# A gated cross-attention and expert layer: the attention groups' work in a new order on all engines

## What is computed

```python
h  = layernorm(x)
q  = rope(h @ Wq.T + bq) * 16**-0.5;  k = rope(ctx @ Wk.T + bk);  v = ctx @ Wv.T + bv
p  = softmax(where(causal and within 128, q @ k.T, -inf))          # for each of 16 heads
x  = x + tanh(g_xattn) * ((p @ v) @ Wo.T + bo)
xf = layernorm(x)
ri = concat(xf, [mean, std, min, max, l2, share of zeros])          # six router statistics
probs = softmax(gelu(ri @ r1_w.T + r1_b) @ r2_w.T)                  # then the best two, capacity 140 an expert
x  = x + tanh(g_ffn) * (sum of the chosen experts' silu MLPs + 0.05 * weighted adapters)
```

## Time and profile before

| | us |
|---|---|
| median of 3 runs | 757.16 (756.15 to 764.54) |
| the profiled execution's own time | 759.58 |
| its span in the profile | 757.7 |
| TensorE matmul busy | 650.4 (86%) |
| VectorE busy | 526.0 (69%) |
| ScalarE busy | 405.2 (53%) |
| GpSimd busy | 323.7 (43%) |

### The profile page before, as it was taken

How to read it: one execution, slowest core, us unless ns; L and a number is a source line. 1 busy time by engine, 2 the same in 40 slices (tenths; PEclk the granted TensorE clock), 3 DMA queues, 4 the chain that set the end, 5 groups by cost and what they waited for, 6 DMA issues and landing times.

```text
span 757.7 us, 17528 instructions
## 1 busy us (share of the span) xinstructions
PE 650.4 (86%) x5275; PEld 513.0 (68%) x5275; DVE 526.0 (69%) x1548; ACT 405.2 (53%) x1569; POOL 323.7 (43%) x340
## 2 busy tenths in 40 slices
PE   8788988989889898899988112899999999999992
PEld 4455655656656566566654101599999999999992
DVE  6765786867778677785988889677778645445441
ACT  2377787887878878788683555022222222222220
POOL 3443462544526435262112000435665665665643
PEclk9999999999999999999798555699999999999997
DMA  5610020200202002010101601169888988888821
GB/s 183 219 37 26 26 74 2 74 27 25 73 0 73 26 25 73 0 49 1 50 2 50 243 0 25 35 200 259 255 250 257 268 260 264 266 236 264 274 44 15
DMA packets 57852, 85.83 MB, mean 113 GB/s; under 512 B 11452, under 2 KB 28468, under 8 KB 57652
## 3 DMA queue, kind: packets, MB, share of 16 engines
q1 hardware_dynamic: 47588, 74.37, 29.7%
q0 software_dynamic: 9216, 9.76, 7.9%
q10 hardware_dynamic: 976, 0.89, 0.4%
HBM read 72.30 MB, written 12.69 MB: 112 GB/s over the span
## 4 chain that ended last, share of the span: by engine, by line
PE 51%; ACT 20%; DVE 17%; issue 7%; DMA 2%; POOL 1%; ACTq 1%; DVEq 1%; POOLq 0%
PE pair L1014 19%; ACT arena L1320 10%; PE bank L1024 10%; DVE arena L1493 4%; PE pair L1655 3%; PE pair L1646 3%; PE bank L1609 2%; ACT arena L583 2%; PE pair L515 2%; PE bank L1036 2%; ACT arena L1269 2%; PE bank L1597 1%; PE pair L1641 1%; PE bank L1003 1%; DVE we L1474 1%
## 5 line engine op out<-in xcount | busy, mean ns | idle before, releaser
L1320 ACT ACTIVATE arena<-pair,arena 112x112 f32<-112x112 f32 x512 | 174.5, 362 | 28.2 <-DVE arena L1493 19.5
L1014 PE MATMUL pair<-arena,we 128*128 128x140 f32 x1024 | 138.0, 283 | 0.7 <-ACT arena L927 0.6
L905 POOL DMA_INDIRECT rows_out<-arena,slot_row x64 | 94.4, 1475 | 95.8 <-DVE arena L958 82.6
L1014 PEld LDWEIGHTS pair<-arena,we 128*128 128x128 f32 x1024 | 128.5, 190 | 1.2 <-issue 1.2
L935 ACT ACTIVATE arena<-pair 128x140 f32<-128x140 f32 x160 | 45.9, 287 | 149.6 <-PE pair L1014 149.6
L970 DVE SCALAR_TENSOR_TENSOR arena<-arena,pair 128x140 f32<-128x140 f32 x160 | 47.5, 297 | 98.4 <-ACT arena L935 97.5
L1320 ACT ACTIVATION_READ_ACCUMULATOR arena<-pair,arena 112x1 f32 x512 | 108.6, 212 | 0.0
L894 POOL DMA_INDIRECT arena<-rows,slot_row x64 | 63.3, 989 | 85.5 <-issue 85.5
L1655 PE MATMUL pair<-tab,arena 112*112 112x112 f32 x512 | 70.2, 274 | 16.7 <-ACT arena L1320 16.6
L1024 PE MATMUL bank<-arena,we 128*128 128x140 f32 x512 | 83.7, 286 | 0.0
L1655 PEld LDWEIGHTS pair<-tab,arena 112*112 112x112 f32 x512 | 50.5, 137 | 41.4 <-ACT arena L1320 25.1
(11 more groups left out here) (214 smaller groups left out, 1196.2 us busy)
## 6 DMA issues: line engine op xcount, KB each, us to landing
we<-w_experts_in SPq DMA_DIRECT2D x192, 256.0 KB, 4.2
wa<-w_adapters_in SPq DMA_DIRECT2D x16, 384.0 KB
arena<-ctx_in SPq DMA_DIRECT2D x8, 448.0 KB, 4.5
arena<-x_in SPq DMA_DIRECT2D x8, 448.0 KB, 3.8
rows_out<-arena SPq DMA_DIRECT2D x8, 448.0 KB, 3.3
rows<-arena SPq DMA_DIRECT2D x8, 448.0 KB, 3.4
arena<-ways_in SPq DMA_DIRECT2D x1, 1024.0 KB, 5.0
arena<-rows,slot_row POOLq DMA_INDIRECT x64, 3.8
```

Source lines behind the costliest of these rows:

```text
L905: nc.gpsimd.indirect_dma_start(d["out"], bass.IndirectOffsetOnAxis(ap=slot_row[:, h, e:e + 1], axis=0), yr[e % 2][:, h, :], None, compute_ ...
L1014: last = nc.tensor.matmul(banks[m % 4][:, part * CAP:(part + 1) * CAP], w[:, col0:col0 + 128], xet[j % 2][:, c, :], start=(c == 0), stop=( ...
L1320: last = nc.scalar.activation(pr[s % 2][:, j, :], banks[BS[s % 4]][0:T, j * T:(j + 1) * T], ACT.Exp, bias=nmx[s // 2 % 2][:, s % 2, j:j + ...
```

## The change

The same operations run in another order, with the waits that go with it. K, X and Q of the next group come some steps later; V moves from the group before into the own group (steps 0 and 3). O comes a step earlier, T0 and S too. Weighing is two steps earlier, the turned sums one (step 6 of a batch, before items are past: `sums` is called at each step behind the items). The inverse is taken two steps earlier and spread ahead of ScalarE's copy of the turned unit. ScalarE reads all banks of items behind the exponentials of the step. VectorE takes the maximum first in a step; its rotations, normalizations and statistics have new steps. X0 and S use the third list's bank, X1 the first's. GpSimd's order is new. In the last group and the tail the logits and the first choices come later, and the tail's hidden rows stand behind S.

```diff
-FRONT = [(0, "K", 0), (2, "K", 1), (3, "V", 0), (4, "X", 0), (5, "X", 1), (6, "Q", 0), (8, "Q", 1), (11, "V", 1)]
+FRONT = [(4, "K", 0), (6, "K", 1), (7, "X", 0), (8, "X", 1), (11, "Q", 0), (12, "Q", 1), (GU, "V", 0), (GU + 3, "V", 1)]
+FIRST_ROWS, KEYS_AND_QUERIES = 2, 6
...
-OUT = [(NU * b + 9, "O", b) for b in range(GB)]
-ROUTE = [(GU + 10, "T", 0), (GU + 11, "T", 1), (GU + 14, "S", 0), (GU + 15, "H", 0)]
+OUT = [(NU * b + 8, "O", b) for b in range(GB)]
+ROUTE = [(GU + 8, "T", 0), (GU + 11, "T", 1), (GU + 13, "S", 0), (GU + 15, "H", 0)]
...
-TURN, WEIGH, DENOM, SUMS, ATT = 2, 7, 6, 7, 8
+TURN, WEIGH, INVERT, DENOM, SUMS, KEEP, ATT = 2, 5, 4, 6, 6, 6, 7
...
-ROTATE = (1, 5, 7, 9)
-EMPTIED = (0, 2)
-LN1_STATS, LN1_APPLY = 0, 2
-LN1_SECOND = (2, 3)
-LN2_STATS, LN2_APPLY = 4, 8
-XF_STATS = {10: ("mean", "min"), 12: ("max", "zeros")}
+ROTATE = (5, 8, 12, 13)
+EMPTIED = (0, 0)
+LN1_STATS, LN1_APPLY = 0, 6
+LN1_SECOND = (2, 6)
+LN2_STATS, LN2_APPLY = 4, 7
+XF_STATS = {8: ("mean",), 10: ("min", "zeros",), 12: ("max",)}
...
-LOGITS = {1: (0, 1), 3: (2, 3), 7: (4, 5), 20: (6,)}
-SHIFTED, RAISED = (3, 7, 22), (4, 8, 22)
+LOGITS = {4: (0, 1), 5: (2, 3), 9: (4, 5), 20: (6,)}
+SHIFTED, RAISED = (5, 9, 22), (6, 10, 22)
-CHOOSE = {5: ((0, 0), (0, 1)), 7: ((0, 2),), 9: ((0, 3), (0, 4)), 13: ((0, 5),), 15: ((0, 6), (1, 0), (1, 1)),
+CHOOSE = {7: ((0, 0), (0, 1)), 8: ((0, 2),), 11: ((0, 3), (0, 4)), 13: ((0, 5),), 15: ((0, 6), (1, 0), (1, 1)),
...
-HIDDEN_ROWS, HIDDEN_BANK = 11, 1
+HIDDEN_ROWS, HIDDEN_BANK = 13, 1
...
+BANK_OF = {("X", 0): 2, ("S", 0): 2}
+EARLY_ITEMS = ()
...
@@ at_step @@
-            if kind == 0:
-                assert when < STEPS
+            if kind == 0 and when < STEPS:
                 hit, back = front and when == s, -1
+            elif kind == 0:
+                hit, back = own and prev and when - STEPS == s, 0
...
@@ GpSimd, group @@
             if front:
                 ln1_rstd(g + 1)
-                rope(g + 1, 1 - par, 0)
             if own:
                 spread(g, par, 2)
+            if prev:
+                ln2_rstd(g - 1)
+            if front:
+                rope(g + 1, 1 - par, 0)
+            if prev:
+                router_stats(g - 1)
+            if own:
+                spread(g, par, 3)
             if front:
                 rope(g + 1, 1 - par, 1)
-                if not own:
-                    spread(g + 1, 1 - par, 0)
-            if prev:
-                ln2_rstd(g - 1)
+                spread(g + 1, 1 - par, 0)
+                add_bias(g + 1, 1 - par)
             if front and own:
                 rope(g + 1, 1 - par, 2)
-            if own:
-                spread(g, par, 3)
-            if front and own:
                 rope(g + 1, 1 - par, 3)
-            if prev:
-                router_stats(g - 1)
-            if front:
-                add_bias(g + 1, 1 - par)
-                if own:
-                    spread(g + 1, 1 - par, 0)
...
@@ ScalarE, items @@
-                if what not in "VO" and (what in "XTS" and s % 2 == 0) == early and not (own and (what, j) == ("K", 0)):
+                if (what not in "VO") and (own and (what, j) in EARLY_ITEMS) == early:
                     item(g - back, (par + back) % 2, kind, what, j, n, front and not own, not front and not own)
-
-            for kind, back, what, j, n in at_step(s, 1, front, own, prev) if own and early else ():
-                if (what, j) == ("K", 0):
-                    item(g - back, (par + back) % 2, kind, what, j, n, False, False)
...
@@ ScalarE, group @@
             for s in range(STEPS):
+                for back, u in unit_at(s, DENOM, own, prev):
+                    if u % NU == 0:
+                        wait(act, s_rden, GB * (g - back) + u // NU + 1)
+                        wait(act, s_rt, GB * (g - back) + u // NU)
+                        nc.scalar.copy(rdenx.rearrange("p (h d) -> p h d", h=NH),
+                                       rden.unsqueeze(2).to_broadcast([T, NH, DH])).then_inc(s_rdx, 1)
                 for back, u in turned_at(s, own, prev):
...
-                items(g, par, s, front, own, prev, True)
...
-                for back, u in unit_at(s, DENOM, own, prev):
...
-                for back, u in unit_at(s, SUMS, own, prev):
+                for back, u in unit_at(s, KEEP, own, prev):
                     if u % NU == 0:
                         wait(act, s_rt, GB * (g - back) + u // NU + 1)
+                        wait(act, s_pv, GB * (g - back) + u // NU + 1)
...
@@ VectorE, group @@
-                for back, u in unit_at(s, DENOM, own, prev):
-                    if u % NU == 0:
-                        wait(dve, s_exp, GU * (g - back) + u + NU)
-                        nc.vector.reciprocal(rden, den[u // NU % 2]).then_inc(s_rden, 1)
+                if own and s % 2 == 0:
+
+                    wait(dve, s_s, GU * g + s + 2)
...
                 for back, u in unit_at(s, ATT, own, prev):
...
-                if own and s % 2 == 0:
...
                 for back, u in turned_at(s, own, prev):
...
+                for back, u in unit_at(s, INVERT, own, prev):
+                    if u % NU == 0:
+                        wait(dve, s_exp, GU * (g - back) + u + NU)
+                        wait(dve, s_rdx, GB * (g - back) + u // NU)
+                        nc.vector.reciprocal(rden, den[u // NU % 2]).then_inc(s_rden, 1)
...
@@ TensorE, item @@
-        def item(q, par, loads, kind, what, j, n, first, tail, between):
-            out = banks[BANKS_FIRST[what, j] if first else BM[kind]]
+        def item(q, par, loads, kind, what, j, n, first, tail, front):
+            out = banks[BANKS_FIRST[what, j] if first else BM[BANK_OF.get((what, j), kind)]]
             if not first:
-                wait(pe, s_mf[kind], FIRST[kind] + len(KINDS[kind]) * q + n)
+                if (what, j) == ("X", 0):
+                    wait(pe, s_mf[2], FIRST[2] + len(ROUTE) * (q - 2))
+                elif (what, j) == ("X", 1):
+                    wait(pe, s_mf[0], FIRST[0] + len(FRONT) * q + FIRST_ROWS)
+                else:
+                    wait(pe, s_mf[kind], FIRST[kind] + len(KINDS[kind]) * q + n)
+                if (what, j) == ("T", 0) and front:
+                    pe.wait_ge(s_mf[0], FIRST[0] + len(FRONT) * (q + 2) + FIRST_ROWS + 1)
...
             elif what == "H":
-                wait(pe, s_xft, 3 * (q + 1))
                 if tail:
                     out = banks[BS[HIDDEN_BANK]]
                 else:
+                    wait(pe, s_xft, 3 * q + 3)
                     hidden_rows(out)
-                between()
+                wait(pe, s_xft, 3 * (q + 1))
...
@@ TensorE, weigh @@
-            if b == 0:
-                wait(pe, s_v, 2 * (q + 1))
+            if b % 2 == 0:
+                wait(pe, s_v, 2 * q + b // 2 + 1)
...
@@ TensorE, turn_sums @@
             wait(pe, s_rdx, GB * q + b + 1)
+            wait(pe, s_att, GB * q + b)
...
@@ TensorE, group @@
+                sums(g, own, prev, s)
                 if not front and own:
                     for early in LOGITS.get(s, ()):
                         early_logits(early)
-                if s != HIDDEN or not prev:
-                    sums(g, own, prev, s)
```

17 lines of the change are left out of this document (6 added, 11 removed).

## The result

The new order is slower: median 776.09 us (762.75 to 782.43, 18 runs) against 759.85 (753.26 to 764.54, 18 runs) for the order before. The ratio is 1.0111 [1.0075, 1.0146]; it leaves out executions more than 1.5% above the fastest, of which the new order has many, so the medians lie further apart (1.021). The profiled execution took 774.29 us, its span is 772.5; before they were 759.58 and 757.7. The forecast was 741, with a range of 730 to 758.

A forecast was written before the change was run, and what follows sets the result against it. TensorE bounds middle groups: 40.3 us of work, 6.4 of stalls from uneven step pairs. Gains 10.8 (middle) + 5.5 (first group) - 0.3 (tail) = 16 us: 759.58 to 743.6, less 2.4 to the median: 741, range 730 to 758.

The forecast's parts named there:

- The chain: Middle groups: dependencies followed through one new group, 43.7 us plus 0.6 for forgotten drains, 44.3 us.
- both at no cost: GpSimd in a group: batch 3's key spread and the bias with the last two rotations finish in time, costing nothing.
- The clock: Middle groups: 0.6 us a group for half a spell more of lowered TensorE clock, at 1.2 us a spell.
- rival C: Middle groups: a 2 us stall before X0 with two more behind lowers TensorE's clock; 754 us, chance 0.07.
- The gain of 1.8 a group: Six middle groups: each 1.8 us shorter than 46.68, 10.8 us in all.
- First full group: First full group: the 3.04 us wait before V0 goes and step 4's scores start earlier; gain 5.5 us.
- Last full group: Last full group: takes on two V, 3.6 us of TensorE; between +3.6 and -3, taken as 0.
- There is room: Last full group: 44.56 us for 34.4 of work at 0.89 of the clock, so added V could be hidden.
- The tail's own account: Tail: S 2.4 us earlier, then 1.7 to 3.35 of hidden rows; between -0.9 and +1.2, taken as +0.3.
- Rivals A: Middle groups: early weighing and early sums wait, 1.55 us in two more places a group; 753 us, chance 0.14.
- B: Middle groups, steps 4 to 9: VectorE's backlog delays X0, a loss beyond 4.4 us of wait; 764 at 5.8, chance 0.11.
- Rival D: Middle groups: TensorE less full than assumed, stalls fall to about 1.5 us, groups to 42.5; 727 us, chance 0.10.

The follow-up runs named there:

- written out: Middle groups as straight code instead of a loop: new order 752.85 us, ratio 0.9938 to the looped order before; order before 753.43 us, 0.9947.
- shift by three: New order, looped, with three thin matmuls (16 columns) ahead of the loop in TensorE's code: 766.14 us, ratio 1.0086 to the order before.
- full fillers: New order, looped, with ten matmuls of 448 columns in the wait before X0: 763.09 us, ratio 1.0053; also used in four other profiled kernels.
- early normalization: New order with the first normalization at step 2 instead of 6 in the middle groups: 769.88 us, ratio 1.0134 to the order before.
- three shifted kernels: New order, looped, with three, ten or twenty-five thin matmuls ahead of the loop: 766.14, 765.06 and 767.62 us.
- the control: The new order unchanged, measured again on the same chip as the kernel with three thin matmuls ahead of the loop: 774.95 us, ratio 1.0183 to the order before.
- the last experiment: New order, middle groups as straight code, ten 448-column fillers before X0, last group's logits and choices spread, hidden rows at step 11: 748.65 us, ratio 0.9868.

## Why the prediction was wrong

- **The chain** (44.3 us for a group, before the clock) was 1.2 to 1.4 short: looped groups of the new order without half clock take 45.5 to 45.7. The waits it named were there: 2.18 before X0 (2.0), 0.64 before the sums where no half clock hides it (0.8), none over 0.24 before a weighing (0.1 taken); of the 1.1 before the turn of unit 9, 0.34 was left. Missed were 0.57 before the turn of unit 3, which put step 6's scores at 6.45 us behind step 4's (6.2 in the other groups) instead of 5.65 (done at 7.07, less 1.42), and 0.8 to 1.4 before the next group's scores. For the latter the chain gave the last rotation 0.2 us of slack and no price for products of VectorE and GpSimd at the same time; "both at no cost" was wrong by this wait, some 1 us a group, of which 0.56 is the meeting of the two engines shown above. Against an old group of 45.90 the order gains 0.2 to 0.4 looped, 0.84 written out, not the 1.6 that 44.3 says.
- **The clock** was the term mis-sized, by what rival C names, the stall before X0. The gain of 1.8 a group is 46.68 less 44.9: the chain's 44.3 and 0.6 for half a spell more, at 1.2 us a spell. No run shows the 0.6; the runs showed in its place 6.8 us at half clock in every middle group of the profile, at a price of 1.7 us. Windows with and without it, same kernel (shift by three):

```profile
113.05:160.26 47.21, 44.04 (x357) 30.27 (x358) 36.16 (x87) 37.31 (x158) 20.95 (x26) 0.93 0.14 41
...
302.11:347.65 45.54, 41.17 (x357) 27.84 (x358) 36.17 (x88) 38.10 (x163) 21.63 (x26) 1.00 0.07 21
```
  1.7 a group, some 10 us in six, where rival C, put at 754, stood for nine more spells of 1.5 us, 13. The error was the size of the term and the chance of C, 0.07: in the trace before all three spells of the middle groups begin behind waits of 1.30, 1.36 and 1.55 us, and a longer one, of 2.0, was foreseen in the same text. That the idle time before X0 brings the spell is shown by the full fillers (none of 30 groups, against 43 of 54) and by the early normalization, which takes the wait away and leaves two spells of 3.4 us in steps 8 and 9, each in a group that begins with a stand. Whether a wait of the same length elsewhere would do the same isn't shown, and 10 us is for the profiled execution: the profile of the shift by three has 6.8 us behind X0 in three groups and 3.4 in one.
- **Stands** were in no rival. In the profiled run there is one, 5.24 us and 2.7 after it at half clock; over many runs they are the 7 to 11 us between the new order (774.95, 776.09) and its three shifted kernels (765.06 to 767.62), 8.8 on the same chip, and about half of its scatter of 20 us (the shifted kernels scatter by 9 to 11). They need no change of the new order's steps to go away, three instructions ahead of the loop do it. Whether the order before would have them if its code lay otherwise wasn't tried.
- **First full group**: -3.8 instead of -5.5. V0's 3.04 us is gone and the scores of step 4 start at 31.36, as foreseen (31.3); but the granted clock is 0.88 in this group, 0.96 before.
- **Last full group and tail.** Together they took 5.8 us more where 0.3 was foreseen, and the 0 for the last full group is the term that was mis-sized. By its own border it is +2.5 here, inside the -3 to +3.6, and +5.6 in the control, outside. From the group's first scores to those of its last pair, step 14, it took 37.29 us before (347.43 to 384.72) and 42.46 after (357.92 to 400.38; 43.12 in the control); 1.2 us of that is a weighing and S, which now stand ahead of these scores. "There is room" was wrong: TensorE's longest wait in the group was 0.76 us before, and now it waits for VectorE and ScalarE five times, 0.73 to 1.78 us:

```profile
392.76 0.56 PE L1649 MATMUL pair<-arena 112*112 112x448 bf16 x2 [1.55 <-DVE we L1494]
...
398.76 0.97 PE L1680 MATMUL bank<-we,arena 112*32 112x112 f32 x32 [1.78 <-DVE we L1494]
```
  Steps 4 and 5 hold O, a weighing and two parts of the logits, 7.21 us (368.49 to 375.70); with these spread over later steps in the last experiment, they took 5.62.
- **The tail's own account** came out about as foreseen. S comes 26.61 us after the last scores (400.38 to 426.99), where before it came 28.71 after them (384.72 to 413.43), so 2.1 earlier (2.4 foreseen); behind it stand the hidden rows at half clock, 2.98 us (427.21 to 430.19, foreseen 1.7 to 3.35), and the first routing turn comes 32.77 us after the last scores instead of 32.15:

```profile
414.29 7.50 PE L521 MATMUL pair<-arena 112*112 112x448 bf16 x24
421.63 0.54 PE L1595 MATMUL bank<-tab,arena 112*128 112x112 f32 x4
...
426.99 0.42 PE L1624 MATMUL bank<-tab,arena 112*128 112x112 f32 x1 [2.21 <-DVEq L1468]
427.21 3.15 PE L1570 MATMUL pair<-we,arena 128*128 128x448 f32 x4
```
  With the hidden rows back ahead of S it was 32.48 us, so their place is worth 0.3 us here.
- **Rivals A, B and D** fell: in the middle groups weighings wait 0.24 us at most, X0 2.2 and not 4.4 (16 us in six groups would have been 4.7), and no middle group of any experiment took under 44.4. Steps 2 and 3 of the order before, which the prediction puts at 5.0 us of work, are 4.5 and the 0.42 us wait before V0; it enters no sum. Rival D, TensorE less full than its matmul busy time says (28.24 us of weight loads beside 42.46), is not borne out: written-out groups at full clock still take 44.8 us with 27.86 us of weight loads.

Together in the middle groups, against -10.8: chain +7.8 (six times 1.3), clock +6.6 (six times 1.7, less the 3.6 counted), a stand with its half clock +7.9, a further spell of half clock in the first middle group (7.50 us from step 0 to 2 instead of 5.87) +1.6. That is 23.9 of the 24.8 that were missed. The steps that failed, in the prediction's own terms, are the chain of 44.3 us, the 0.6 for the clock and the 0 for the last full group; the stand was no term at all. On the whole program the stands are the largest part: without them (the kernels with moved code) the new order still takes 765 to 768 us, 24 to 27 more than the forecast, so clock, chain and last group would have made it wrong by themselves.

## What to carry to other kernels

When a change makes one wait longer in a stretch where TensorE is nearly full, compare it with the waits behind which the trace before already has a spell of half clock (here 1.30 to 1.55 us), and price a spell in nearly every pass (here 43 of 54); full-width fillers in that wait took it away here, but 2.5 us was all that the program gained by it, since other spells came. Before judging a reordering inside a hardware loop, move the loop's code by a few instructions or write it out: three idle instructions changed this kernel by 9 us, the order itself, written out, by less than 1. Read the first and the last pass apart from the middle ones: here the middle of the new order is better and its end is 9.4 us worse. Where the border between two stretches moves, compare their sum. And where a chain ends with less than half a microsecond of slack, look for products of VectorE and GpSimd at the same time on the way to it, which here made 1.56 us of 0.60.

## What was not expected of the hardware

- A jump back over some 95 us of TensorE's code costs nothing that shows (the order before, scores at 160.29 and 253.91 without a wait), or TensorE stands 5.2 to 7.4 us and 9 packets of instructions come over the next trip; moving the loop by three instructions was enough to go from the one to the other, and at one place it can come at one jump and not at the other.
- With ten matmuls of 448 columns in a wait of 2 us no fall of the granted clock to 0.50 began within 2.3 us of X0's start, in 30 groups; with ten of 16 columns it began there in five groups of six, and with none in 43 of 54.
- VectorE's product of two SBUF operands: 0.60 us alone, 1.56 beside GpSimd's product of 1.14. The other way round, a GpSimd product that met one of VectorE's took 1.52 us (written out, at 288.78) instead of 1.14.
